# Routing worked into the attention steps of a gated cross-attention and mixture-of-experts block

## The chip, the cores and the metric

One core of a Trainium2 chip runs the whole block. The metric is device time in microseconds (us) of one launch. Each engine (PE is the matrix engine, DVE the vector engine, ACT the scalar engine, POOL is GpSimd, SP issues DMAs) runs its own list of instructions strictly in order, and the engines meet only at semaphores.

## The reference, cut to what matters

```
x = x + tanh(g_xattn) * cross_attention(layernorm(x), ctx, Wq, Wk, Wv, Wu, bu, q/k norm weights)
x = x + tanh(g_ffn)   * moe(layernorm(x), Wg, W1, b1, W2, b2, Ws1, bs1, Ws2, bs2)

cross_attention: q, k, v = projections to 16 heads x 64; q and k are layer-normed per head;
                 softmax(q k^T / 8) v per sequence of 64; then the output projection and bu
moe:             probs = softmax(h @ Wg); the 2 best of 8 experts, weights normalised to sum 1
                 out = sum of weight * (silu(h @ W1[e] + b1[e]) @ W2[e] + b2[e])
                       + 0.1 * (silu(h @ Ws1 + bs1) @ Ws2 + bs2)
```

There are 64 sequences of 64 tokens, so 4096 tokens, in 32 tiles of 128. The model width is 128, the hidden width of an expert 512, all in float32; a projection is three matmuls (high x high, high x low, low x high) with operands split into parts.

## The kernel before, in words

**Attention steps.** The loop `steps` runs `step(s)` for s from -5 to 36 on four engines, written out in full. In one step each engine works on several tiles at once, shifted by a few steps: PE transposes q and k of tile s, takes its scores, and attends to tile s-1. The order inside a step is the order of the calls in that engine's `step`; nothing else schedules it. Names used below: `project_v(j, t)` is half j of the value projection of tile t, three matmuls on L981 to L983; `transpose_probabilities(j, t)` (L1017) turns the softmax of tile t and waits for POOL's `normalise_rows(t)` (L588) through `p_ready`; `values` (L399) copies v out of PSUM on ACT; `high_part` (L360) and `low_part` (L560) split the tokens; `expert_weights` on ACT (L427) rounds a slice of W1 to its high part, and `expert_weights` on POOL (L600) subtracts it for the low part, waiting through `w1hi_ready`; `second_rstd` (L546, L548) and `newton_step` (L573 to L582) make inverse roots for the norms; `scale` (L715) on DVE applies them before the transposes of q and k; `residual` (L691) adds the attention result to x and frees PE's bank (`y_read`).

**W1.** In step 1 ACT issues the DMAs of all of W1, W2 and the shared expert's weights (L346 to L352). The slices of W1 are split on ACT in call `expert_weights(s + 2)` and on POOL in call `expert_weights(s - 3)` of the same step: POOL asks for a slice that ACT has done five steps ago.

**Group stage.** After the last attention step 8 groups of 4 tiles follow (`group`). For each: second norm (L773), transposes (L1110), logits in split parts (L1118), softmax and choice of two experts by some 35 small DVE operations, the rank of each token among those of its expert (L1146 to L1149), row copies (L860), and 8 indirect DMAs on POOL (L627) that scatter the rows into `routed`. The row buffer has two slots, so DVE waits for the scatters of two groups ago (`f_sent`). The shared expert runs beside it (L1125 to L1137 on PE, L467 on ACT, L795 and L797 on DVE).

**Routed stage.** From the counts DVE works out a schedule of 39 row tiles of 256 rows, each of one expert; SP loads them, PE runs them (first hidden matmul L1176), POOL scatters results, and a last part gathers and adds them.

## Time and profile before

| what | us |
|---|---|
| median of 3 runs | 764.32 (762.17 to 764.89) |
| the profiled execution | 764.29 |
| its span, first to last instruction | 762.5 |
| first softmax transpose to the last attention step's, tiles 0 to 31 | 63 to 428 |
| groups of the router and shared expert | about 440 to 563 |
| first to last routed tile | about 582 to 740 |

A profile row gives the start, the busy time, the engine, the source line, the operation with what it writes and reads, and in square brackets how long the engine had been idle and what released it. The mean granted clock of PE over the span is 0.913 of full speed.

### The profile page before, as it was taken

The numbers are of one execution on the slowest core, as the hardware profiler recorded it, in microseconds if no ns is written. First come the engines' busy times: TensorE is split into PE (matmuls) and PEld (weight loads), VectorE is DVE, ScalarE is ACT, GpSimd is POOL, SyncE is SP. The second block draws the span as 40 slices with busy tenths as digits, with TensorE's granted clock in tenths as the row PEclk, the third lists the DMA queues.
The fourth block names the chain that finished last, engine by engine and source line by source line (L and its number), as shares of the span: only waits on it lengthen the run. The fifth ranks groups of instructions, "written<-read, shape, count | busy, mean of one in ns | idle before, by whom it ended". The sixth has DMA issues, their size and how long they took to land.

```text
span 762.5 us, 21522 instructions
## 1 busy us (share of the span) xinstructions
PE 613.7 (80%) x7702; PEld 532.5 (70%) x7702; DVE 482.2 (63%) x1189; ACT 457.1 (60%) x964; POOL 365.3 (48%) x712
## 2 busy tenths in 40 slices
PE   1718989999999999999998579786834998988860
PEld 0517777777787787877877567675733998988860
DVE  4635877878887888888877366654552444444327
ACT  3517787878888888888888233433312454444425
POOL 3422455555655555556555234555452554544450
PEclk9978999999999999999999768888865999999995
DMA  7062000000000000000000040111024222222218
GB/s 251 32 224 54 3 30 3 3 29 3 30 3 2 30 3 30 3 4 2 3 1 3 2 78 28 36 39 38 28 66 74 70 68 67 74 71 67 64 48 325
DMA packets 30037, 37.90 MB, mean 50 GB/s; under 512 B 4992, under 2 KB 20624, under 8 KB 29808
## 3 DMA queue, kind: packets, MB, share of 16 engines
q1 hardware_dynamic: 20800, 21.42, 9.2%
q0 software_dynamic: 4720, 9.89, 3.9%
q10 hardware_dynamic: 4416, 5.25, 2.5%
q8 instruction: 62, 1.02, 0.6%
q14 instruction: 39, 0.32, 0.1%
HBM read 23.13 MB, written 13.42 MB: 48 GB/s over the span
## 4 chain that ended last, share of the span: by engine, by line
PE 56%; DVE 11%; ACT 11%; issue 8%; another core or an unknown queue 5%; POOL 3%; DMA 3%; ACTq 2%; SPq 0%; DVEq 0%; POOLq 0%
PE ps L1008 8%; PE ps L1190 8%; PE ps L981 6%; PE ps L983 5%; PE ps L982 5%; PE ps L1017 4%; PE ps L1034 4%; ACT prob L406 4%; PE ps L1049 4%; PE ps L1178 3%; PE ps L1176 3%; ACT qk_T L391 3%; PE ps L1177 3%; ACTq L351 1%
## 5 line engine op out<-in xcount | busy, mean ns | idle before, releaser
L644 POOL DMA_INDIRECT results<-spo,xs_ix x78 | 75.8, 972 | 87.3 <-DVE spo L955 70.8
L708 DVE TENSOR_REDUCE ss<-wide 128x16 f32<-128x1024 f32 x64 | 78.1, 1220 | 58.5 <-ACT wide L367 48.3
L496 ACT ACTIVATE qk_T<-ps,b_cols 128x256 f32<-128x256 f32 x156 | 61.8, 474 | 77.0 <-PE ps L1178 75.5
L391 ACT ACTIVATE qk_T<-ps,lnw 128x512 f32<-128x512 f32 x128 | 96.8, 788 | 14.4 <-issue 13.1
L981 PE MATMUL ps<-w_hi,xc_hi 128*128 128x512 f32 x192 | 91.1, 475 | 13.7 <-POOL xc_lo L560 9.6
L1008 PE MATMUL ps<-ident,wide 128*128 128x128 f32 x512 | 75.9, 281 | 30.7 <-ACT qk_T L391 29.9
L1008 PEld LDWEIGHTS ps<-ident,wide 128*128 128x128 f32 x512 | 57.7, 142 | 56.9 <-ACT qk_T L391 43.0
L627 POOL DMA_INDIRECT routed<-w_raw,slot x64 | 62.2, 971 | 70.6 <-issue 53.0
L715 DVE TENSOR_TENSOR wide<-ps,rstd 128x512 f32<-128x512 f32 x128 | 81.6, 679 | 2.9 <-POOL rstd L582 2.8
L367 ACT ACTIVATE wide<-ps 128x512 f32<-128x512 f32 x128 | 77.3, 606 | 7.1 <-PE ps L983 7.1
L983 PE MATMUL ps<-w_hi,xc_lo 128*128 128x512 f32 x192 | 77.2, 402 | 0.0
L982 PE MATMUL ps<-w_lo,xc_hi 128*128 128x512 f32 x192 | 76.8, 400 | 0.0
L1190 PE MATMUL ps<-w_sb,qk_T 128*128 x624 | 76.0, 275 | 0.0
L1190 PEld LDWEIGHTS ps<-w_sb,qk_T 128*128 128x128 f32 x624 | 72.9, 192 | 0.0
L1063 PEld LDWEIGHTS ps<-wu_sb,spo 128*128 128x128 f32 x512 | 63.5, 196 | 5.3 <-ACT spo L421 2.8
L1063 PE MATMUL ps<-wu_sb,spo 128*128 128x128 f32 x512 | 64.2, 280 | 2.5 <-ACT spo L421 2.5
L588 POOL TENSOR_TENSOR prob<-prob,rinv 128x1024 f32<-128x1024 f32 x32 | 61.0, 1906 | 9.2 <-DVE rinv L744 9.2
L1176 PE MATMUL ps<-w_lo,w_hi 128*128 128x256 f32 x156 | 49.6, 318 | 10.1 <-DVE w_lo L926 10.1
L926 DVE TENSOR_TENSOR w_lo<-ps,w_lo 128x256 fp32r<-128x256 f32 x39 | 16.6, 425 | 59.4 <-ACT w_lo L487 48.7
L981 PEld LDWEIGHTS ps<-w_hi,xc_hi 128*128 128x128 f32 x192 | 37.1, 193 | 20.9 <-DVE w_lo L671 11.2
L737 DVE TENSOR_REDUCE sm<-prob 128x16 f32<-128x1024 f32 x32 | 39.1, 1221 | 17.6 <-ACT prob L406 17.6
L560 POOL TENSOR_TENSOR xc_lo<-xc_in,xc_hi 128x256 fp32r<-128x256 f32 x32 | 24.1, 754 | 52.9 <-ACT xc_hi L360 52.9
(175 smaller groups left out, 1445.6 us busy)
## 6 DMA issues: line engine op xcount, KB each, us to landing
v_sb<-routed SPq DMA_DIRECT2D x39, 129.0 KB
xc_in<-in_x SPq DMA_DIRECT2D x8, 256.0 KB, 2.8
xc_in<-in_ctx SPq DMA_DIRECT2D x8, 256.0 KB, 3.2
w_raw<-in_L_ffn_W ACTq DMA_DIRECT2D x1, 2048.0 KB, 9.2
wide<-results SPq DMA_DIRECT2D x4, 512.0 KB, 4.8
w_raw<-results SPq DMA_DIRECT2D x4, 512.0 KB, 8.2
out_x<-x_res SPq DMA_DIRECT2D x8, 256.0 KB, 4.1
x_res<-in_x SPq DMA_DIRECT2D x1, 1792.0 KB, 8.6
```

The lines of the kernel that those rows point to most:

```text
L367: nc.scalar.activation(sq[:, n, j * 512:j * 512 + 512], ps[2 * n + j][:, :], ACT.Square, scale=HD ** -0.5).then_inc(sq_ready[n][j], 1)
L391: nc.scalar.activation(qk_T[:, n, 4 * j:4 * j + 4, :].rearrange("p a n -> p (a n)"), ps[6 + j][:, :], ACT.Identity, bias=lnw[:, 2 * n + 1: ...
L644: gp_.indirect_dma_start(out=results[:, :], out_offset=bass.IndirectOffsetOnAxis(ap=xs_ix[:, b4, a:a + 1], axis=0), in_=yb[:, b4, a, :], i ...
L708: nc.vector.tensor_reduce(ss[:, n, :], sq[:, n, :].rearrange("p (h d) -> p h d", h=HEADS), AX.X, ALU.add).then_inc(ss_ready[n], 1)
L715: nc.vector.tensor_tensor(qk_n[:, n, j * 512:(j + 1) * 512].rearrange("p (h d) -> p h d", h=8), ps[2 * n + j][:, :].rearrange("p (h d) -> ...
L981: nc.tensor.matmul(out_bank, xc_hi[:, t % 2, src, :], w_hi[:, w, cols[j]], start=True, stop=False)
L982: nc.tensor.matmul(out_bank, xc_hi[:, t % 2, src, :], w_lo[:, w, cols[j]], start=False, stop=False)
L983: return nc.tensor.matmul(out_bank, xc_lo[:, t % 2, src, :], w_hi[:, w, cols[j]], start=False, stop=True)
L1008: last = nc.tensor.transpose(ps[6 + j][:, a * P:(a + 1) * P], qk_n[:, n, c0:c0 + P], ident[:, :])
L1063: last = nc.tensor.matmul(ps[7][:, 0:D], o_T[:, p, :, :].rearrange("p b n -> p (b n)"), wu_sb[:, p, :], start=(p == 0), stop=(p == PAIRS - 1))
L1176: nc.tensor.matmul(h, w_hi_c, xs_hi[:, n % 2, :], start=True, stop=False)
L1190: last_ = nc.tensor.matmul(ps[4 + n % 2][:, a * D:(a + 1) * D], hT[:, n % 2, c, a * P:(a + 1) * P], w2e[:, c, :], start=(c == 0), stop=(c ...
```

## The change

The second norm, the transposes, the logits, the choice of experts and the scatters leave the group stage and become calls inside the attention steps; routing works on batches of 8 tiles (`BT`), three batches inside the steps and the fourth after them. Rows have 130 columns instead of 129, and all 32 tiles of them are kept (`rows_all`), so no slot is waited for. The logits use one float32 matmul of a tile. The token parts have four slots (`XD`) instead of two. W1 is loaded by SP expert by expert into two slots and split in 27 parts, in steps 3 to 29. The shared expert has a stage of its own, straight-line, beginning in step 32. The calls inside each `step` stand in another order on all four engines.

```diff
@@ ACT
-            for at in w1_slices(s, s):
-                nc.scalar.activation(w1_hi_cols[:, at], w1_raw_cols[:, at], ACT.Copy).then_inc(w1hi_ready, 1)
+            e, cols = w1_part(s)
+            sc.wait_ge(w1_in[e % 2], 16 * (e // 2 + 1))
+            nc.scalar.activation(w1_hi[:, e, cols], w1_raw[:, e % 2, cols], ACT.Copy).then_inc(w1hi_ready, 1)
...
             def step(s):
...
+                values(1, s)
+                high_part(s + 4)
+                expert_weights(s)
                 probabilities(0, s - 1)
                 probabilities(1, s - 1)
-                expert_weights(s + 2)
...
@@ POOL
             def expert_weights(s):
                 if s in W1_STEPS:
-                    gp_.wait_ge(w1hi_ready, s - (STEADY.start - 1))
+                    e, cols = w1_part(s)
+                    gp_.wait_ge(w1hi_ready, s - W1_FIRST + 1)
...
+            def scatter(t):
+                if has(t):
+                    gp_.wait_ge(f_slot, t // BT + 1)
+                    for c in range(2):
+                        gp_.indirect_dma_start(out=routed[:, :], ...
...
             def step(s):
-                variance(0, s)
-                newton_step(0, s)
-                normalise_rows(s - 2)
-                output_bias(s + 1)
+                scatter(s - SCATTER_LAG)
                 variance(1, s)
                 newton_step(1, s)
-                expert_weights(s - 3)
+                output_bias(s - 2)
+                token_eps(s + 1)
+                expert_weights(s)
+                low_part(s + 3)
                 second_rstd(s - 3)
...
+                variance(0, s + 1)
+                newton_step(0, s + 1)
+                normalise_rows(s - 1)
@@ DVE
             def step(s):
+                sum_squares(0, s + 1)
+                scale(1, 0, s)
+                row_sums(s - 1)
+                row_inverses(s - 1)
+                route(s, 12)
...
                 residual(s - 2)
...
@@ PE
             def step(s):
...
+                transpose_probabilities(0, s - 1, before_p)
+                transpose_probabilities(1, s - 1, before_p)
+                scores(s)
+                attend(s - 1)
...
+                project_qk(1, 0, s + 2)
+                transpose_qk(1, 1, s + 1, before_k)
+                project_v(1, s + 1)
+                project_qk(0, 0, s + 3)
...
+            shared_result(0)
+            for g in range(1, GROUPS):
+                if g + 2 < GROUPS:
+                    transpose_tokens(g + 2)
+                if g + 1 < GROUPS:
+                    shared_hidden(g + 1)
+                if g == 1:
+                    ranks(NB - 1)
+                shared_result(g)
@@ SP
+            def load_expert(e):
+                if e >= 2:
+                    sp.wait_ge(ffw_ready, len(W1_PARTS) * (e - 1))
+                sp.dma_start(w1_raw[:, e % 2, :], w1[e, :, :] if e < E else ws1).then_inc(w1_in[e % 2], 16)
```

`route(s, 12)` on DVE runs, for a batch, 2 small operations in the first of five successive steps, then 8, 6, 12 and 4, each waiting for the one before it; the batches lie in steps 12 to 16, 20 to 24 and 28 to 32.

On PE, the end of one step and the beginning of what follows. In the kernel before, the last two projections of a step's middle are followed by the transposes of the softmax (`ps<-ident,prob`):

```order
L1008 MATMUL ps<-ident,wide 128x128 [waits kn_ready1,y_read]
L1008 MATMUL ps<-ident,wide 128x128 x3
L981 MATMUL ps<-w_hi,xc_hi 128x512 [waits kn_ready0,xlo_ready]
L982 MATMUL ps<-w_lo,xc_hi 128x512
L983 MATMUL ps<-w_hi,xc_lo 128x512
L981 MATMUL ps<-w_hi,xc_hi 128x512 [waits qn_ready0,xlo_ready]
L982 MATMUL ps<-w_lo,xc_hi 128x512
L983 MATMUL ps<-w_hi,xc_lo 128x512
L1017 MATMUL ps<-ident,prob 128x128 [waits p_ready,kT_ready0]
```

There the first projection is of k and the value projections come much earlier in the step. The same place in the changed kernel, where the first three matmuls after the transposes are `project_v(1, s + 1)`:

```order
L1052 MATMUL ps<-ident,wide 128x128 [waits kn_ready1,y_read]
L1052 MATMUL ps<-ident,wide 128x128 x3
L1020 MATMUL ps<-w_hi,xc_hi 128x512 [waits lg_ready]
L1021 MATMUL ps<-w_lo,xc_hi 128x512
L1022 MATMUL ps<-w_hi,xc_lo 128x512
L1020 MATMUL ps<-w_hi,xc_hi 128x512 [waits qn_ready0,xlo_ready]
L1021 MATMUL ps<-w_lo,xc_hi 128x512
L1022 MATMUL ps<-w_hi,xc_lo 128x512
L1061 MATMUL ps<-ident,prob 128x128 [waits p_ready,kT_ready0]
```

The value projection of half 1 has moved to the end of the step, one projection ahead of the softmax transposes.

On ACT, around the split of W1 (`w1_hi`). Before, it follows the two copies of the transposed softmax (`spo<-ps`):

```order
L399 ACTIVATE v_sb<-ps4 128x512 [waits o_done1,v_done0]
L367 ACTIVATE wide<-ps3 128x512 [waits ss_ready1,k_done1]
L391 ACTIVATE qk_T<-ps6,lnw 128x512 [waits s_done,kt_done0]
L391 ACTIVATE qk_T<-ps7,lnw 128x512 [waits s_done,kt_done1]
L367 ACTIVATE wide<-ps2 128x512 [waits ss_ready1,k_done0]
L413 ACTIVATE spo<-ps6 128x512 [waits o_done1,pt_done0]
L413 ACTIVATE spo<-ps7 128x512 [waits o_done1,pt_done1]
L427 ACTIVATE w1_hi<-w1_raw 128x160 [waits ffw_in]
```

The same place on ACT in the changed kernel:

```order
L383 ACTIVATE qk_T<-ps6,lnw 128x512 [waits s_done,kt_done0]
L359 ACTIVATE wide<-ps2 128x512 [waits ss_ready1,k_done0]
L383 ACTIVATE qk_T<-ps7,lnw 128x512 [waits s_done,kt_done1]
L391 ACTIVATE v_sb<-ps5 128x512 [waits o_done1,v_done1]
L352 ACTIVATE xc_hi<-xc_in 128x256 [waits v_done1,c_loaded1]
L419 ACTIVATE w1_hi<-w1_raw 128x176 [waits w1_in0]
L405 ACTIVATE spo<-ps6 128x512 [waits o_done1,pt_done0]
L405 ACTIVATE spo<-ps7 128x512 [waits o_done1,pt_done1]
```

The split now stands behind the copy of v, half 1, and ahead of the copies of the softmax.

On POOL, around its half of the split (`w1_lo`) and the scaling of the softmax rows (`prob<-prob,rinv`). Before:

```order
L588 TENSOR_TENSOR prob<-prob,rinv 128x1024 [waits rinv_ready]
L594 TENSOR_TENSOR x_res<-x_res,tgbu 128x128 [waits bn_done,tgbu_ready]
L568 TENSOR_SCALAR var_eps<-ss,eps 128x16 [waits ss_ready1]
L573 TENSOR_TENSOR newton<-root 128x16 [waits root_ready1]
L575 TENSOR_TENSOR newton<-newton,var_eps 128x16 [waits nw_step1]
L577 TENSOR_SCALAR newton<-newton 128x16 [waits nw_step1]
L582 TENSOR_TENSOR rstd<-root,newton 128x16 [waits kn_ready1,kn_ready0,nw_step1]
L600 TENSOR_TENSOR w1_lo<-w1_raw,w1_hi 128x160 [waits w1hi_ready]
```

The changed kernel, from its half of the split to the scaling of the rows:

```order
L609 TENSOR_TENSOR w1_lo<-w1_raw,w1_hi 128x176 [waits w1hi_ready]
L569 TENSOR_TENSOR xc_lo<-xc_in,xc_hi 128x256 [waits xhi_ready]
L555 TENSOR_TENSOR ve_2<-mv_2,eps 128x1 [waits mv2_ready]
L557 TENSOR_TENSOR rstd_2<-ve_2,expo 128x1 [waits ve2_ready]
L577 TENSOR_SCALAR var_eps<-ss,eps_q 128x16 [waits epsq_ready,ss_ready0]
L582 TENSOR_TENSOR newton<-root 128x16 [waits root_ready0]
L584 TENSOR_TENSOR newton<-newton,var_eps 128x16 [waits nw_step0]
L586 TENSOR_SCALAR newton<-newton 128x16 [waits nw_step0]
L591 TENSOR_TENSOR rstd<-root,newton 128x16 [waits qn_ready1,qn_ready0,nw_step0]
L597 TENSOR_TENSOR prob<-prob,rinv 128x1024 [waits rinv_ready]
```

The row scaling that PE's next step begins with now stands behind POOL's half of the split in the same call of `step`, with eight operations between them; before, it stood ahead of it.

## Rows read from the trace of the kernel before

**Rows 1.** Windows: busy time per engine (count), granted clock, DMA share, GB/s.

```profile
core 0: us, PE busy (x) PEld busy (x) DVE busy (x) ACT busy (x) POOL busy (x), PEclk, DMA share, GB/s
200.00:300.00 100.00, 96.09 (x1595) 80.01 (x1586) 82.77 (x144) 85.11 (x179) 57.56 (x146) 1.00 0.04 13
440.00:563.00 123.00, 95.15 (x574) 83.16 (x572) 69.68 (x365) 45.12 (x63) 58.08 (x62) 0.78 0.15 42
```

**Rows 2.** Timeline of PE in one attention step.

```profile
203.89 1.98 PEld L1063 LDWEIGHTS ps<-wu_sb,spo 128*128 128x128 f32 x16
...
209.11 0.39 PE L982 MATMUL ps<-w_lo,xc_hi 128*128 128x512 f32 x1
...
209.34 0.40 PE L983 MATMUL ps<-w_hi,xc_lo 128*128 128x512 f32 x1
...
209.70 0.85 PEld L1017 LDWEIGHTS ps<-ident,prob 128*128 128x128 f32 x8 [0.40 <-issue]
...
210.72 1.16 PE L1034 MATMUL ps<-qk_T 64*64 64x64 f32 x64
...
211.71 1.11 PE L1049 MATMUL ps<-spo,v_sb 64*64 64x64 f32 x64
```

**Rows 3.** Timeline of the same step, ACT and what it waits for.

```profile
203.89 0.39 PE L983 MATMUL ps<-w_hi,xc_lo 128*128 128x512 f32 x1
...
204.38 0.42 ACT L360 ACTIVATE xc_hi<-xc_in 128x256 fp32r<-128x256 f32 x1 [0.99 <-PE ps L983]
...
207.09 0.59 ACT L399 ACTIVATE v_sb<-ps 128x512 f32<-128x512 f32 x1
...
210.39 1.08 ACT L413 ACTIVATE spo<-ps 128x512 f32<-128x512 f32 x2 [0.40 <-PE ps L1017]
...
211.37 0.34 ACT L427 ACTIVATE w_hi<-w_raw 128x160 fp32r<-128x160 f32 x1
```

**Rows 4.** Timeline of POOL in the same steps.

```profile
202.02 0.53 POOL L600 TENSOR_TENSOR w_lo<-w_raw,w_hi 128x160 fp32r<-128x160 f32 x1
...
202.78 0.57 POOL L548 TENSOR_TENSOR rstd<-ve,expo 128x1 f32<-128x1 f32 x1
...
204.88 0.73 POOL L560 TENSOR_TENSOR xc_lo<-xc_in,xc_hi 128x256 fp32r<-128x256 f32 x1 [1.24 <-ACT xc_hi L360]
...
205.59 0.33 POOL L568 TENSOR_SCALAR var_eps<-ss,eps_q 128x16 f32<-128x16 f32 x1
...
206.61 0.22 POOL L573 TENSOR_TENSOR newton<-root 128x16 f32<-128x16 f32 x1 [0.69 <-ACT root L382]
...
207.50 0.22 POOL L582 TENSOR_TENSOR rstd<-root,newton 128x16 f32<-128x16 f32 x1
...
207.68 1.91 POOL L588 TENSOR_TENSOR prob<-prob,rinv 128x1024 f32<-128x1024 f32 x1
...
219.45 1.91 POOL L588 TENSOR_TENSOR prob<-prob,rinv 128x1024 f32<-128x1024 f32 x1
```

**Rows 5.** Windows after three long waits of PE, columns as in rows 1.

```profile
429.00:437.00 8.00, 6.00 (x83) 5.35 (x81) 0.00 (x0) 2.05 (x4) 0.00 (x0) 0.51 0.01 2
548.70:551.80 3.10, 3.10 (x8) 2.44 (x9) 1.63 (x4) 0.00 (x0) 0.00 (x0) 0.50 0.07 21
582.70:589.20 6.50, 5.95 (x26) 5.37 (x27) 1.61 (x4) 2.93 (x8) 0.00 (x0) 0.50 0.26 61
```

**Rows 6.** Timeline: a small DVE operation of the router.

```profile
460.77 0.22 DVE L880 TENSOR_REDUCE w_raw<-w_raw 128x8 f32<-128x64 f32 x1
```

**Rows 7.** Timeline: ACT's queue held by a DMA issue in step 1.

```profile
45.80 11.18 ACTq L351 DMA_DIRECT2D w_sb<-in_L_ffn_Ws  x1
```

**Rows 8.** Timeline from the second last softmax transpose to the first routed tile.

```profile
418.74 1.06 PE L1017 MATMUL ps<-ident,prob 128*128 128x128 f32 x8 [0.72 <-POOL prob L588]
...
454.04 3.65 PEld L1137 LDWEIGHTS ps<-w_sb,wide 128*128 128x128 f32 x32 [0.64 <-ACT wide L467]
...
463.47 0.99 POOL L627 DMA_INDIRECT routed<-w_raw,slot  x1 [0.30 <-issue]
...
584.38 0.58 PE L1176 MATMUL ps<-w_lo,w_hi 128*128 128x256 f32 x1
```

**Rows 9.** Groups of instructions, window 444 to 563: count, busy, mean ns, idle before.

```profile
L795 DVE SCALAR_TENSOR_TENSOR prob<-ps,tg,x_res 128x512 f32<-128x512 f32 x7 | 5.3, 751 | 33.5 <-remote 32.6 <-PE ps L1137 0.9
```

More of the change, by code:

```diff
@@ L27 @@
 GN = GT * P
-ROW = D + 1
+ROW = D + 2
+BT = 8
+NB = TILES // BT
+XD = 4
 RT = 256
@@ L254, in eps_of, with batch_at @@
             return eps_q[:, t % 4:t % 4 + 1] if n == 0 else eps[:, 1, 0:1]
-        def groups(eng, group):
-            for g in range(2):
-                group(g, g, False)
-            with eng.Fori(0, GROUPS // 2 - 2) as i:
-                for half in range(2):
-                    group(2 * i + (2 + half), half, False)
-            for g in range(GROUPS - 2, GROUPS):
-                group(g, g % 2, g == GROUPS - 1)
+        def batch_at(s, lag):
+            b, at = divmod(s - lag, BT)
+            return (b, at) if 0 <= b < NB - 1 else (None, 0)
         def r_slot(n):
@@ new lines, in logits, with ranks @@
+            def logits(t):
+                if has(t):
+                    if has(t + 4):
+                        pe.wait_ge(sub_ready[1], t + 5)
+                    else:
+                        pe.wait_ge(lg_ready, t)
+                    if t == 0:
+                        pe.wait_ge(wg_in, 16)
+                    pe.wait_ge(rT_ready, t + 1)
+                    nc.tensor.matmul(ps[5][:, 0:E], row_T[:, t % 2, :], wg_raw[:, :], start=True, stop=True).then_inc(lg_done, 1)
+            def ranks(b):
+                pe.wait_ge(f_cnt, b + 1)
+                nc.tensor.matmul(ps[5][:, E:2 * E], before[:, :], cnt_b[:, b, :], start=True, stop=True)
+                nc.tensor.matmul(ps[5][:, 2 * E:3 * E], ones_b[:, :], cnt_b[:, b, :], start=True, stop=True).then_inc(f_rank, 1)
@@ new lines, in route_ranks, with transpose_tokens @@
+            def route_ranks(s, lag):
+                b, at = batch_at(s, lag)
+                if b is not None and at == 3:
+                    ranks(b)
+            def transpose_tokens(g):
+                pe.wait_ge(norm_ready, GT * g + GT)
+                if g == 0:
+                    pe.wait_ge(sub_ready[0], TILES)
+                else:
+                    pe.wait_ge(f_lo, g)
+                for j in range(GT):
+                    last = nc.tensor.transpose(ps[4][:, j * P:(j + 1) * P], rows_all[:, GT * g + j, 0:D], ident[:, :])
+                last.then_inc(f_t, 1)
@@ new lines, in shared_result @@
+            def shared_result(g):
+                pe.wait_ge(act_ready, CH * (g + 1))
+                if g >= 1:
+                    pe.wait_ge(f_x2, 2 * g - 1)
+                else:
+                    pe.wait_ge(o_ready[0], TILES)
+                for j in range(GT):
+                    for c in range(CH):
+                        last = nc.tensor.matmul(ps[6][:, j * D:(j + 1) * D], act[:, g % 2, c, j * P:(j + 1) * P], w2_sb[:, E, c, :],
+                                                start=(c == 0), stop=(c == CH - 1))
+                last.then_inc(fy_done, 1)
@@ L1151, in _ @@
-            transpose_tokens(0, 0)
-            pe.wait_ge(ffw_ready, len(W1_STEPS) + 2)
-            pe.wait_ge(w2_in, 3 * 16)
-            pe.wait_ge(y_read, TILES)
-            logits(0)
-            groups(pe, group)
+                project_qk(0, 1, s + 2)
+                transpose_qk(0, 0, s + 1, before_q)
+                logits(s - 4)
+                route_ranks(s, 12)
+                transpose_qk(0, 1, s + 1, before_q)
+                project_qk(1, 1, s + 2)
+                project_v(0, s + 1)
```

625 lines of the change are left out of this document (322 added, 303 removed).

## Prediction

> **What bounds the kernel now.** I read the windows first. In the attention steps PE is busy 96 of 100 us at full clock, DVE 83, ACT 85, POOL 58; in the group stage PE is busy 95 of 123 us at a granted clock of 0.78 [rows 1]. So PE bounds the first stage and something else the second. The timeline gives the pace of the first: POOL's row scaling comes again after 219.45 - 207.68 = 11.77 us [rows 4]. For the second, the groups of instructions say what is late: DVE sat idle 33.5 us ahead of the shared expert's sum, 32.6 of them released by nothing on the core, which are the scatters of two groups before [rows 9]. A scatter takes 0.99 us and the next follows 0.30 later, 1.3 us each [rows 8], so the 64 of them are 83 us of the stage. From the second last softmax transpose (tile 30, at 418.74) to the first routed hidden matmul (584.38) pass 165.6 us [rows 8]. That stretch is what the change attacks.
>
> **Part 1: the stage after attention.** What stays in it is PE's work for the shared expert. A hidden layer is 12 matmuls 0.23 us apart (209.11 to 209.34) [rows 2], 2.8 us. A result is 3.65 us [rows 8], four transposes are 0.4 (8 in 0.85) [rows 2]. After tile 30's transposes come: the rest of its step, 7 us of PE; transposes, high and low part of the first group, and its hidden layer, 6; then tile 31's softmax, attention, projection and the norm and logits of the last tiles, a chain over ACT, DVE and PE of some 10. That is 23. From there 8 results, 6 hidden layers and 5 times four transposes are 29.2 + 16.8 + 2.0 = 48 us. DVE has the last batch to route in between: 32 small operations of about 0.25 (0.22 for one [rows 6], plus the hand-over), the clearing of the pads (3 to 4 us, on POOL before), the schedule (6), so it holds PE by some 8 us at results 1 to 3: 56. The hand-over to the first routed tile is 3 (a sum on DVE, a transpose, its two parts). 23 + 56 + 3 = 82 against 165.6, **-84 us**. POOL's remaining scatters don't set the end: 16 of the last batch after its places, 38 us in, take 21, with landing and loading the rows 65 of the 82. At both ends: PE's pauses there might cost clock, 15 us (-69); if DVE holds nobody, -95. The stretch from tile 28 to 30 gets 2 longer (three tiles at the end of the loop ran at less than 11.77), and the first routed tiles no longer start at clock 0.50, which stood for 6.5 us [rows 5], worth -3. Taken: **-85**.
>
> **Part 2: the wait that the new order makes.** This is where I expect the result to be decided. POOL's `expert_weights(s)` asks for the slice that ACT splits in its own `expert_weights(s)`. In ACT's step s this stands behind `values(1, s)`, which needs `project_v(1, s)`, and PE does that almost at the end of its step s-1. In POOL's step s it stands ahead of `normalise_rows(s - 1)`, and PE's step s begins with waiting for those rows. `low_part(s + 3)`, next to it, asks for a part that ACT made one step earlier, `high_part(s + 4)`; the split has no such distance. Before, ACT was five steps ahead. So in steps 3 to 29 PE's last value projection and its next softmax transposes are joined by a chain that nothing can overlap, since both ends are PE's own and everything between is in order. Its length, in the order in which it runs:
> - end of the projection to ACT's copy: 0.10 (203.89 + 0.39 to 204.38); the copy 0.49 (one takes 0.59, two 1.08); `high_part` 0.33 (0.42 less the same overlap of 0.09); the split 0.36 (0.34 for 160 columns, now up to 176) and 0.08 to POOL, as between L360 and L560: 1.36 [rows 3, 4].
> - POOL: its split and the first operation of `second_rstd` 0.80 (202.02 to 202.78, and 0.04 for the columns); `low_part` 0.71 (204.88 to 205.59); the power 0.60; `variance` 0.33; Newton 0.89 (206.61 to 207.50) and 0.18; the row scaling 1.91 and 0.11 to PE (to 209.70): 5.53 [rows 2, 4].
>
> Together 6.9 us. Only one projection lies in it, and it too waits until POOL's Newton and DVE's `scale` are through. PE's own part, from the softmax transposes to the end of the value projection, is 0.85 + 1.0 scores + 1.05 attention + 5 projections at 0.69 and 0.17 of drain + 16 transposes 1.7 + the output projection 1.98 + new: one transpose 0.11 and the logits 0.25, and 0.1 for a drain on ACT = 10.65 [rows 2]. A step is 17.5 us instead of 11.77. **27 x 5.75 = +155.** The bounds are tight, since each term is a row: 147 to 165. Outside steps 3 to 29 PE needs 11.3 us with its new work where it had some 1 us of pauses in 11.77; I take nothing for it.
>
> **Part 3: PE's clock.** In each such step PE now waits 5.6 us, runs one projection, and waits another 0.4. After long waits the clock stood at half: 0.50 for 3.1 us of work from 548.7, for 6.5 us from 582.7, 0.51 for the 8 us from 429 [rows 5]. With pauses under 1 us it is 1.00 [rows 1]. The projection starts the work 1.2 us ahead of the transposes, so 1.9 to 5.3 us of the step proper run at half, which costs half of that, 0.95 to 2.65; I take the middle, 1.9 with the projection's own share. **27 x 1.9 = +51**, with 0 and 75 as ends. The Trainium skill, in "TensorE: Matmul & The Clock Gate", section "HAM oscillation — how this bites in real kernels", says that an array that waits between bursts starts every burst throttled and that the penalty is half of the throttled time. By that rule this term is there in every one of the 27 steps; by the attention rows alone, which never leave 1.00, it would be 0.
>
> **Part 4: routing inside the steps.** DVE runs 2, 8, 6, 12 and 4 small chained operations of 0.25 us in five steps of a batch [rows 6], ahead of `residual`, which PE waits for before `transpose_qk(1, 1, ...)`. The cover there is about 0.5 us (the residual can be done at 8.7 of the step, PE asks at 9.3). What sticks out: 0, 1.5, 1.0, 2.5 and 0.5 = 5.5 a batch, three batches, **+16** (12 to 22). It lies ahead of the value projection, so the wait of part 2 doesn't hide it. The scatters (two a step, 2.6 us on POOL) and the row and logit copies are hidden: POOL and DVE stand still for over 5 us in each of these steps anyway. Without part 2 they would matter: POOL's 58% plus 22% is still under PE.
>
> **Part 5: W1 by SP.** ACT's queue is held 11.18 us in step 1 by a DMA issue behind 4.6 MB of weights [rows 7], and PE waits. Half of the bytes leave that queue. Between 0 and -9 us; taken **-5**.
>
> **Sum**, on the profiled execution's 764.3 us (span 762.5, 1.8 around it; it is the median of the runs): 764.3 - 85 + 155 + 51 + 16 - 5 = **896 us**.
>
> **Rivals.**
> - *The wait isn't there*, because the step counters of ACT and POOL don't line up as I read them, and the steps stay at about 11.6 us. Then 764.3 - 85 + 16 - 5 = 690 us, and the change wins clearly. It decides if ACT's split comes over 7 us ahead of PE's softmax transposes. For it: POOL and ACT have slack in the profile and everything else in the new order lines up within a step. Against it: the waits and the order above say otherwise. 0.07.
> - *The clock stays up*: the projection inside the pause is enough work to hold 1.00. 845 us. For it: 0.7 us of full-rate matmul after 5.6 of pause; against it the 0.50 after pauses of 3 us at the end of attention. 0.20.
> - *The clock doesn't come back within a step*, as from 429 to 437 [rows 5]. PE's 10.65 us are then nearly doubled, where ACT doesn't hold it anyway: some 8 more per step instead of 1.9, 1060 us. 0.05.
>
> **How the numbers follow.** My forecast has 0.68. The range takes in the second rival at its upper bounds and the ends of part 3: 840 to 940. A measurement of this kernel can tell 0.5% from no change. Faster by that: the first rival, 0.07; the same 0.01, as no case lies near 764; slower 0.92.
>
> **What would show it.** In the profile after: POOL's split of W1 idle before it for over 4 us, released by ACT's split; PE's softmax transposes idle before them with POOL's row scaling as releaser, 27 times; the row scaling every 17.5 to 20 us in steps 3 to 29 and about 11.5 in the two after; PE's clock in the steps between 0.7 and 0.9; the stretch from tile 30's transposes to the first routed tile near 82 us. If the row scaling comes every 12 us, part 2 is wrong and the kernel is faster. If the pace is 17.5, part 3 is.

## The result, and the profile after

The changed kernel takes 905.57 us (median of 4 runs, 902.04 to 908.83) against 763.25 for the kernel before on the same chip: a ratio of 1.188, with a 95% interval of 1.184 to 1.192. Forecast were 896 us and a range of 840 to 940. The profiled execution took 908.83 us with a span of 907.1.

Windows of the changed kernel; columns as in [rows 1], the length of the window behind its bounds:

```profile
200.00:300.00 100.00, 70.03 (x1033) 59.08 (x1034) 53.58 (x114) 55.02 (x116) 34.41 (x88) 0.84 0.04 12
625.09:728.85 103.76, 74.15 (x647) 66.46 (x645) 44.87 (x118) 36.92 (x60) 35.20 (x38) 0.89 0.18 46
```

In the attention steps PE was busy 96 of 100 us at full clock [rows 1]; now 70 at 0.84, and every other engine is down with it. No engine has become the bound: something holds all of them in turn. The second window reaches from tile 30's softmax transposes to the first routed hidden matmul. It is 103.8 us where it was 165.6 [rows 8]. With these marks the two spans can be taken apart exactly: up to tile 30's transposes 625.09 - 418.74 = **+206.4 us**, from there to the first routed tile 103.8 - 165.6 = **-61.9**, the rest 178.3 against 178.1, **+0.1**. Together +144.6, the difference of the spans.

The timeline shows what holds the engines. This is the changed kernel at the end of one PE step, between PE's last value projection and its next softmax transposes, to be laid beside [rows 3, 4]:

```profile
229.54 0.40 PE L1022 MATMUL ps<-w_hi,xc_lo 128*128 128x512 f32 x1
229.99 0.60 ACT L391 ACTIVATE v_sb<-ps 128x512 f32<-128x512 f32 x1
230.47 0.42 ACT L352 ACTIVATE xc_hi<-xc_in 128x256 fp32r<-128x256 f32 x1
230.78 0.34 ACT L419 ACTIVATE w_hi<-w_raw 128x160 fp32r<-128x160 f32 x1
231.20 0.52 POOL L609 TENSOR_TENSOR w_lo<-w_raw,w_hi 128x160 fp32r<-128x160 f32 x1 [8.68 <-ACT w_hi L419]
231.68 0.73 POOL L569 TENSOR_TENSOR xc_lo<-xc_in,xc_hi 128x256 fp32r<-128x256 f32 x1
...
233.19 0.33 POOL L577 TENSOR_SCALAR var_eps<-ss,eps_q 128x16 f32<-128x16 f32 x1
...
234.39 0.22 POOL L591 TENSOR_TENSOR rstd<-root,newton 128x16 f32<-128x16 f32 x1
234.57 1.90 POOL L597 TENSOR_TENSOR prob<-prob,rinv 128x1024 f32<-128x1024 f32 x1
234.64 0.69 DVE L713 TENSOR_TENSOR wide<-ps,rstd 128x512 f32<-128x512 f32 x1 [6.59 <-POOL rstd L591]
...
235.48 0.77 PE L1020 MATMUL ps<-w_hi,xc_hi 128*128 128x512 f32 x1 [5.55 <-DVE wide L713]
...
236.90 0.84 PE L1061 MATMUL ps<-ident,prob 128*128 128x128 f32 x3
```

Read the starts downwards: the projection ends at 229.94, ACT copies it out, rounds the tokens, rounds W1's slice; POOL had been idle 8.68 us until just that came, and goes through its list to the row scaling; the transposes follow at 236.90. From end to start that is 6.96 us, and up to the row scaling these steps come one behind the other. The row scaling ends at 236.47; the last 0.4 us up to the transposes are the query projection of PE itself, which began at 235.48. The bracket on PE names DVE's scaling as releaser, and DVE's names POOL's Newton result: the profile names the last link of a chain each time, and only POOL's bracket names the link that was new.

Groups of the changed kernel over the whole span (line, engine, operation, count, then busy us and mean ns, then idle before and its releasers) show how often:

```profile
L609 POOL TENSOR_TENSOR w_lo<-w_raw,w_hi 128x176 fp32r<-128x176 f32 (+1 forms) x27 | 14.7, 544 | 242.2 <-ACT w_hi L419 242.2
L1020 PE MATMUL ps<-w_hi,xc_hi 128*128 128x512 f32 x192 | 99.2, 517 | 162.4 <-DVE wide L713 153.2 <-POOL xc_lo L569 9.2
L1061 PE MATMUL ps<-ident,prob 128*128 128x128 f32 x256 | 59.0, 409 | 5.7 <-ACT qk_T L383 5.6
```

It happens 27 times, one for each slice. The step can be read from the row scaling, which in [rows 4] came again after 11.77 us:

```profile
215.32 1.90 POOL L597 TENSOR_TENSOR prob<-prob,rinv 128x1024 f32<-128x1024 f32 x1
234.57 1.90 POOL L597 TENSOR_TENSOR prob<-prob,rinv 128x1024 f32<-128x1024 f32 x1
```

19.25 us here. Plain steps take 18.3 to 19.7 us (mean 18.9 over the second to the eleventh), longer where the half clock lasts longer; steps with routing take 19.1 to 22.2, and the three behind the 27th slice take 12.9, 14.9 and 15.7, with the third batch's routing in them.

### The profile page after: what moved, and what is told of

It is laid out like the page before. It is cut to its first block, busy times and chain, and to the rows that moved or that the text cites. A ratio compares the mean times of both kernels' runs of the same rounds, so it can differ in the third digit from the quotient of the medians.

```text
span 907.1 us, 21117 instructions
## 1 busy us (share of the span) xinstructions
PE 646.7 (71%) x7614; PEld 563.9 (62%) x7614; DVE 469.9 (52%) x1043; ACT 456.4 (50%) x980; POOL 360.8 (40%) x705
## 4 chain that ended last, share of the span: by engine, by line
PE 55%; DVE 15%; POOL 10%; issue 7%; ACT 7%; another core or an unknown queue 3%; DMA 1%; ACTq 1%; POOLq 0%; DVEq 0%; SPq 0%
PE ps L1274 7%; PE ps L1061 6%; PE ps L1078 6%; PE ps L1020 5%; PE ps L1052 4%; PE ps L1108 4%; PE ps L1022 4%; PE ps L1021 4%; DVE wide L713 3%; PE ps L1093 3%; PE ps L1260 2%; PE ps L1262 2%; PE ps L1176 2%; POOL xc_lo L569 2%
## 5 line engine op out<-in xcount | busy, mean ns | idle before, releaser
L1020 PE MATMUL ps<-w_hi,xc_hi 128*128 128x512 f32 x192 | 99.2, 517 | 162.4 <-DVE wide L713 153.2
L713 DVE TENSOR_TENSOR wide<-ps,rstd 128x512 f32<-128x512 f32 x128 | 87.6, 685 | 177.8 <-POOL rstd L591 177.8
L1020 PEld LDWEIGHTS ps<-w_hi,xc_hi 128*128 128x128 f32 x192 | 40.0, 208 | 180.8 <-issue 166.1
L405 ACT ACTIVATE spo<-ps 128x512 f32<-128x512 f32 x64 | 38.0, 598 | 197.3 <-PE ps L1061 196.9
L609 POOL TENSOR_TENSOR w_lo<-w_raw,w_hi 128x176 fp32r<-128x176 f32 (+1 forms) x27 | 14.7, 544 | 242.2 <-ACT w_hi L419 242.2
L504 ACT ACTIVATE qk_T<-ps,b_cols 128x256 f32<-128x256 f32 x156 | 61.9, 475 | 79.5 <-PE ps L1262 70.9
L1052 PE MATMUL ps<-ident,wide 128*128 128x128 f32 x512 | 80.0, 283 | 19.3 <-DVE x_res L689 17.9
L1022 PE MATMUL ps<-w_hi,xc_lo 128*128 128x512 f32 x192 | 84.3, 439 | 0.0
L706 DVE TENSOR_REDUCE ss<-wide 128x16 f32<-128x1024 f32 x64 | 77.5, 1212 | 12.9 <-ACT wide L359 12.3
L1021 PE MATMUL ps<-w_lo,xc_hi 128*128 128x512 f32 x192 | 83.9, 437 | 0.0
L359 ACT ACTIVATE wide<-ps 128x512 f32<-128x512 f32 x128 | 76.2, 596 | 12.7 <-issue 7.1
L721 DVE TENSOR_REDUCE mx<-ps 128x8 f32<-128x512 f32 x64 | 41.2, 686 | 72.2 <-PE ps L1078 72.2
L615 POOL DMA_INDIRECT routed<-rows_all,slot x64 | 64.4, 1007 | 22.5 <-issue 16.5
L1061 PE MATMUL ps<-ident,prob 128*128 128x128 f32 x256 | 59.0, 409 | 5.7 <-ACT qk_T L383 5.6
L1061 PEld LDWEIGHTS ps<-ident,prob 128*128 128x128 f32 x256 | 52.3, 218 | 16.6 <-ACT qk_T L383 6.5
```

The costliest lines, as they stand in the source:

```text
L359: nc.scalar.activation(sq[:, n, j * 512:j * 512 + 512], ps[2 * n + j][:, :], ACT.Square, scale=HD ** -0.5).then_inc(sq_ready[n][j], 1)
L706: nc.vector.tensor_reduce(ss[:, n, :], sq[:, n, :].rearrange("p (h d) -> p h d", h=HEADS), AX.X, ALU.add).then_inc(ss_ready[n], 1)
L713: nc.vector.tensor_tensor(qk_n[:, n, j * 512:(j + 1) * 512].rearrange("p (h d) -> p h d", h=8), ps[2 * n + j][:, :].rearrange("p (h d) -> ...
L1020: nc.tensor.matmul(out_bank, xc_hi[:, t % XD, src, :], w_hi[:, w, cols[j]], start=True, stop=False)
L1021: nc.tensor.matmul(out_bank, xc_hi[:, t % XD, src, :], w_lo[:, w, cols[j]], start=False, stop=False)
L1022: return nc.tensor.matmul(out_bank, xc_lo[:, t % XD, src, :], w_hi[:, w, cols[j]], start=False, stop=True)
```

## The experiments

The theory: in one step, POOL waits for what ACT makes in the same step behind PE's last product of the step before, ahead of what PE needs first (theory A of the first run). The rivals: the steps are long because of the work moved into them; and, for the sizes, that the clock or the routing carries another share than I gave it. Chips differ here, so every run is compared with the kernel before on its own chip. That one took 763 us in the comparison above (whether on the same chip as the next is not known), 755 in the first four runs, 718 in the next four and 716 in the last four; why is a question of its own, below.

**One step of distance put back**

```diff
@@ POOL, step
-                expert_weights(s)
+                expert_weights(s - 1)
```

> The changed kernel with one number changed: in POOL's step s the subtraction that makes W1's low part takes the slice of step s - 1, which ACT split a whole step earlier, instead of that of step s. Theory A (the same-step hand-over ACT to POOL costs the 27 steps): the row scaling comes every 11.6 to 12.5 us in steps 3 to 29, PE's clock in the windows from 200 to 400 is 1.00, POOL's idle time ahead of the subtraction falls from 242 us to under 20, and the time is about 905 - 155 - 51 = 700 us (690 to 725). Theory B (the steps are long because of what else was moved into them: routing, transposes, logits, scatters): 880 us or more, and the pace stays above 17 us. Theory C (the wait goes, but a second one of the new order stands right behind it): 740 to 850 us.

721.14 us, 0.954 of the kernel before (0.947 to 0.961). The changed kernel would be at 1.188 x 755 = 897 us on this chip, an estimate: it was not run there. The profiles agree with it: behind the last row scaling the changed kernel takes 273.5 us in the first comparison and these four runs take 265 to 267, 8 less, as the kernel before is 8 us faster here. So the one number is worth about 176 us. The group of POOL's split and that of PE's projection in this kernel:

```profile
L609 POOL TENSOR_TENSOR w_lo<-w_raw,w_hi 128x176 fp32r<-128x176 f32 (+1 forms) x27 | 14.9, 551 | 0.0
L1020 PE MATMUL ps<-w_hi,xc_hi 128*128 128x512 f32 x192 | 90.8, 473 | 13.8 <-POOL xc_lo L569 9.2 <-DVE wide L713 3.8 <-issue 0.4
```

242.2 us of idle time have become 0.0, and PE's 153.2 behind DVE have become 3.8. Before the first batch is routed the row scaling comes every 11.2 us in most steps. Theory A holds, with 721 us inside its 690 to 725; the rival, that the moved work makes the steps long, is out: the same work is there. The steps with routing, though, now take 12.9 to 16.9 us, of which later.

**The pause filled**

```diff
+            def filler(s):
+                if s + 1 in W1_STEPS:
+                    pe.wait_ge(v_ready[1], s + 2)
+                    for _ in range(18):
+                        nc.tensor.matmul(ps[5][:, :], w_hi[:, 2, 0:P], w_hi[:, 2, cols[1]], start=True, stop=True)
...
                 project_v(1, s + 1)
+                filler(s)
                 project_qk(0, 0, s + 3)
```

> The changed kernel, with 18 matmuls more on PE (0.23 us each at full clock, into a bank that nobody reads, work that the kernel does not need) between the last value projection's hand-over and the first query projection, in each of the 27 steps, so that the pause of 5.6 us is filled but not shortened. Theory A (part 3 of the prediction: the half clock behind the pause costs 1.9 us a step): granted clock above 0.95 in the windows from 200 to 400, first transposes behind the row scaling at 0.85 us instead of 1.9, time 905 - 51 = 855 us (845 to 870). Theory B (the clock is low but what waits behind those matmuls is not PE): clock near 1.00, time within 8 us of 905. Theory C (the added matmuls run at half clock themselves, 8.3 us instead of 4.1, and stick out of the pause): over 905, up to 990 us.

873.89 us, 1.157 (1.149 to 1.165): 23 us less than 897, a smaller gain than theory A gave with its 845 to 870 us. The clock in the windows of 100 us from 100 to 600 is 1.00, 0.97, 1.00, 1.00 and 0.95, where it was 0.80 to 0.84. First PE behind such a pause in the changed kernel, then the same lines in this one:

```profile
216.23 0.76 PE L1020 MATMUL ps<-w_hi,xc_hi 128*128 128x512 f32 x1 [5.59 <-DVE wide L713]
...
217.65 1.91 PE L1061 MATMUL ps<-ident,prob 128*128 128x128 f32 x8
219.48 1.95 PE L1078 MATMUL ps<-qk_T 64*64 64x64 f32 x64
```

```profile
111.87 4.36 PE L1206 MATMUL ps<-w_hi 128*128 128x512 f32 x18 [0.70 <-ACT v_sb L391]
116.74 0.47 PE L1020 MATMUL ps<-w_hi,xc_hi 128*128 128x512 f32 x1 [0.51 <-DVE wide L713]
...
117.87 1.06 PE L1061 MATMUL ps<-ident,prob 128*128 128x128 f32 x8 [0.20 <-POOL prob L597]
118.86 1.16 PE L1078 MATMUL ps<-qk_T 64*64 64x64 f32 x64
...
122.00 0.46 PE L1093 MATMUL ps<-spo,v_sb 64*64 64x64 f32 x14 [1.18 <-issue]
```

The added matmuls (L1206) leave the wait in place and take the clock from half to full: transposes and scores together take 2.2 instead of 3.9 us. Six of the ten plain steps take 17.3 to 17.4 us, against a mean of 18.9, so the clock costs up to 1.5 us a step, 27 x 1.5 = 40. The other four take 17.7 to 18.8, and in three of them PE stands idle for 0.7 to 1.2 us at an "issue" (the last row), of which the changed kernel has one in the same time. That may be a price of the experiment, which gives PE 972 more instructions (486 matmuls and as many weight loads), but no run shows it: the last run below, which adds none, has 6.0 us of the same waits. The last row scaling starts 27.9 us earlier (605.7 against 633.6), or 23.8 earlier than in the repetition of the changed kernel below (629.5). So the clock is worth 24 to 28 us as measured, and up to 40 if those waits and all else above 17.4 us are the experiment's own. The wait itself is what is left: 17.4 against 11.2 us in the run above.

**Routing behind the residual sum**

```diff
@@ DVE, step
+                if s != TILES:
+                    residual(s - 2)
                 route(s, 12)
                 if s == TILES:
                     lo_part(0)
-                residual(s - 2)
-                if s == TILES:
+                    residual(s - 2)
                     lo_part(1)
```

> The changed kernel with DVE's routing operations of a step placed behind the residual sum instead of ahead of it, all else as it is, the same-step wait too. Theory A (part 4: the routing holds the residual, and so PE, in the steps in which it runs): the four or five steps of a batch fall to about the pace of plain steps (18.3 to 19.3 us), 905 - 16 = 889 us (883 to 895). Theory B (behind the residual the same operations hold the scaling of the next queries instead): within 4 us of 905, and the steps of a batch stay at 20 to 22 us.

880.44 us, 1.165 (1.157 to 1.174), 16.6 less than 897. By the last row scaling the gain is 22.8 us (610.8 against 633.6), or 18.7 against the repetition. The steps with routing fall from 19.1 to 22.2 us to 18.3 to 19.9. PE's waits for DVE's residual sum, 17.9 us between 60 and 640 us in the changed kernel, are gone, and nothing longer has come in their place, since the operations now lie in the time in which DVE waits for POOL anyway (6.59 us at 234.64 above).

**Both edits**

> Both edits of the two experiments, the low part of W1 one step later on POOL and the routing behind the residual sum on DVE. If the two costs add, 700 - 16 = 684 us (675 to 700), and faster than the kernel before by some 80 us. If the routing is hidden by the wait of part 2 in one and sticks out in the other, the difference between this and the first alone shows it: 0 if it costs nothing without the wait, up to 22 us.

705.39 us, 0.933 (0.926 to 0.940), 15.7 less than the first edit alone, 14.9 by the last row scaling. So the order is worth about the same with and without the wait. But it is not all that routing costs. What PE waits for most in the window from 180 to 260 us, in the run with the distance alone and then with both edits (in us, in total, times, longest):

```profile
PE ps L1052 <- DVE x_res L689: 11.0, 4, 3.7
```

```profile
PE ps L1021 <- DVE wide L713: 9.2, 4, 3.4
```

Behind the residual sum the same operations hold the scaling of the queries. The steps of the first batch take 12.2, 15.1, 13.5, 16.3 and 13.0 us in this kernel, plain early ones 11.2; DVE is busy 89 of 100 us in the window from 200 to 300, and little place is left to hide them.

**Padding behind the scatters; scatters held; one scatter moved**

```diff
@@ first: SP
             sp.wait_ge(pad_ready, 2)
+            sp.wait_ge(f_sent, 16 * 2 * TILES)
@@ second: POOL, behind the steps
+            gp_.wait_ge(fy_done, GROUPS)
             for t in range(LAST_STEP - SCATTER_LAG + 1, TILES):
                 scatter(t)
@@ third: POOL, step; scatter(t, (0,)) sends the first choice's row, (1,) the second's
-                scatter(s - SCATTER_LAG)
...
                 second_rstd(s - 3)
+                scatter(s - SCATTER_LAG, (0,))
                 variance(0, s + 1)
                 newton_step(0, s + 1)
                 normalise_rows(s - 1)
+                scatter(s - SCATTER_LAG, (1,))
```

These three start from the version with both edits. They were to find the reason for something in the stage after attention. In the changed kernel's profile PE, ACT and DVE stand still there twice: for 5.44, 8.96 and 3.22 us the first time, and for 11.80, 18.49 and 10.59 us the second, the last 10.6 of them together, while POOL goes on with its scatters. From its chain of waits, and, for the first time, from its timeline:

```profile
658.43 8.94 another core or an unknown queue
...
682.33 10.73 another core or an unknown queue
```

```profile
665.47 5.21 PE L1176 MATMUL ps<-w_sb,wide 128*128 128x128 f32 x32 [5.44 <-issue]
667.39 0.60 ACT L450 ACTIVATE w_lo<-ps 128x512 fp32r<-128x512 f32 x1 [8.96 <-remote]
```

> On the version with both edits: SP waits for all scatters before it sends the padding, so that the padding (nine transfers, 17 us of SP's queue) no longer runs beside the second half of the shared expert's stage. There PE, ACT and DVE stand still for 10.65 us at 487.40, released by nothing that the trace shows, while the padding is under way; an earlier piece of 8.78 us at 463.68 has only scatters beside it. Theory A (the padding's transfers hold what the three engines wait for): the second piece goes or falls under 3 us, the first stays, the first routed tile starts up to 10 us earlier, unless the padding now ends later than PE's shared expert does: 695 to 702 against 705 us. Theory B (the scatters do it): both pieces stay, 705 us or a few more. Theory C (neither, it is the engines' own programs at these places): both pieces stay at the same instructions.

> On the version with both edits: POOL waits for the last shared result before it sends the 26 scatters that stand behind the steps, so none of them runs beside the shared expert's stage; the padding does. Theory B (scatters hold the engines): both unexplained pieces (8.8 and 10.7 us) go, PE's shared stage is 19 us shorter, and then 26 x 1.27 = 33 us of scatters are waited for: 705 - 19 + 33 = 719 us. Theory A (padding): only the second goes, about 728. Theory C: both stay, 738 us or more.

> On the version with both edits: of the two scatters that POOL sends ahead of its first variance in a step, one is moved to the middle of the step, where POOL waits 1.2 to 1.5 us for the sum of squares. Plain steps with scatters take 12.0 us and those without them 11.2. Theory A (the scatters hold POOL's Newton step, and so DVE's scaling): the later steps fall to 11.4 to 11.6, 705 - 8 = 697 us (693 to 701). Theory B (they are hidden, DVE's own load sets 12.0): within 3 us of 705.

These three ran on another chip, on which the kernel before takes 718 us. Measured: 676.51 (0.943, 0.937 to 0.949), 712.12 (0.992, 0.989 to 0.995) and 676.43 (0.945, 0.940 to 0.950). None of the three profiles has a single such piece, the two that still have scatters or padding beside the shared expert included. So these runs could not tell the theories apart, and all three were beside the point: none of them allowed that the pieces would be missing without any of the moves. The repetition below gives the value to compare with, 0.945. Against it, padding moved and one scatter moved are no difference that can be measured, and holding 26 scatters costs (0.992 - 0.945) x 718 = 34 us, which is near their 26 x 1.27 = 33: it shows that they are well hidden where they are.

**Routing spread**

```diff
@@ DVE, route, batches at 2, 3, 5, 6, 6, 6 and 4 operations
                 if at == 1:
                     expert_probabilities(b)
+                if at == 2:
                     choose(0, gp)
-                if at == 2:
+                if at == 3:
                     second_choice(b)
-                if at == 3:
+                if at == 4:
                     count(b)
+                if at == 5:
                     weigh(b)
-                if at == 4:
+                if at == 6:
                     place(b)
```

The batches now take seven steps, so the scatters come two steps later (`SCATTER_LAG` 19 instead of 17).

> On the version with both edits: the routing of a batch, 2, 8, 6, 12 and 4 small DVE operations in five steps of eight, is spread as 2, 3, 5, 6, 6, 6 and 4 over seven, the scatters two steps later. The routing steps now take 12.2, 15.1, 13.5, 16.3 and 13.0 us, the plain ones between 12.0. Theory A (each step has some slack on DVE, 1 us or so, which only the long groups exceed): the steps of a batch fall to 12.5 to 13.5, 705 - 15 = 690 us (683 to 695). Theory B (DVE is full at 12.0, so every operation costs its whole time wherever it stands): within 4 us of 705.

673.06 us, 0.940 (0.937 to 0.943), against 0.945 (0.942 to 0.948): about 4 us, less than the gain of theory A (10 to 22 us) and at the edge of B; the two intervals overlap, so it is not clear of noise. The steps of a batch became 12.2, 12.2, 13.0, 13.7, 13.5, 13.4 and 12.9, 91.0 in sum: the peaks are gone, and the others have grown. The same seven steps take 91.2 in the repetition of both edits below. So what DVE is given here it mostly pays, wherever it stands.

**The changed kernel, and both edits, again**

> The changed kernel again, unaltered, as the neighbour of the three others. On a chip on which the kernel before takes 717 us its seven unexplained pieces (5.14, 4.96, 5.31, 4.47, 5.38, 6.72 and 2.02 us, 34 in all, in the profile shown) should be missing; the changed kernel has four of them in its second stage (8.94, 10.73, 3.78 and 3.80, 27 us). If the pieces belong to the chip or to what else runs on it, the ratio is then about (905 - 27) / (763 - 34) = 1.20 and the pieces are gone; if they belong to the program, they are there on every chip and the ratio stays 1.188.

> The version with both edits again, unaltered (0.9327 of the kernel before, with unexplained pieces of 8.78 and 10.65 us, on a chip where that one took 755 us). Padding moved, one scatter moved and routing spread each gave 0.943, 0.945 and 0.940 on another chip where it took 718. If the pieces belong to the chip, this one is at 0.95 to 0.955 there, and the pieces are gone; if moving the padding did it, they are here again.

872.44 us, 1.219 (1.215 to 1.222), and 675.72, 0.945 (0.942 to 0.948), where the kernel before takes 716. Neither profile has such a piece. The attention steps are the same as on the first chip (the last row scaling starts at 629.5 us instead of 633.6); the stretch to the first routed tile is shorter by 18.9 us, and the two pieces that it lost are 19.7:

```profile
621.22:706.10 84.88, 70.07 (x648) 62.41 (x646) 44.40 (x118) 37.18 (x60) 34.95 (x38) 0.96 0.22 56
```

So the pieces belong to the chip, or to what else goes on there, and not to the program. The kernel before has seven of them, 34 us, all in its group stage, in the only profile there is of it; it is 47 us faster on these chips. The other 13 us fit as well: behind the first routed tile the changed kernel takes 165.2 us in the repetition instead of 178.3, and 763.3 - 34.0 - 13.1 = 716.2, where 716.0 was measured. That the pieces of the kernel before are gone there is such a sum and was not seen.

**All moves together**: the version with both edits, the routing spread, one scatter moved, and W2 and the shared expert's weights loaded by SP instead of ACT.

```diff
@@ ACT, load_experts
-                sc.dma_start(w2_sb[:, 0:E, :, :]. ...
-                sc.dma_start(w2_sb[:, E, :, :], ...
-                sc.dma_start(bs1_sb[:, :], bs1).then_inc(w2_in, 16)
@@ SP, in the loop over the tiles
+                if s == 1:
+                    sp.dma_start(w2_sb[:, 0:E, :, :]. ...
...
```

> Both edits, one scatter of two moved to the middle of POOL's step, routing spread over seven steps, and the loads of W2 and the shared expert's weights issued by SP in place of ACT. The spread took 434.9 - 428.3 = 6.6 us off the end of the attention steps, the scatter 0.4; ACT's square waits 7.1 us for its own engine's DMA issue in step 1, and PE 5.6 us behind that. If the loads are free on SP, that goes too: e4_both_again less 6.6 - 0.4 - 5.6 = 12.6 us (10 to 14). If SP, held by 4.6 MB in its queue, brings tokens or W1 late, the gain is 7 or less.

668.24 us, 0.934 (0.931 to 0.936), 7.5 less than both edits alone; expected were 10 to 14, and 7 or less if SP brought tokens or W1 late. From the first row scaling to the second it now takes 10.7 us instead of 18 to 19, so the held queue of [rows 7] is gone whole. Up to the last row scaling it gains 9.1 us (421.2 against 430.3), and from there to the end it takes 6 us more (245.6 against 239.7). With the routing spread alone that end takes 243.1, so a good half of the 6 goes with the spread, by which the last batches' places and scatters come later; that this is the reason was not tried.

**ACT's split first**

```diff
@@ ACT, step
             def step(s):
...
+                expert_weights(s)
                 square(1, 1, s + 1)
...
                 high_part(s + 4)
-                expert_weights(s)
```

> The changed kernel with ACT's split of W1 at the beginning of its step, ahead of the squares and of the value copy, and POOL's part unmoved (the same step, the same slice). Theory A (not the shared slice as such costs the time, but that ACT's split stands behind the copy that needs PE's last projection): the wait goes and the time is that of the lag put back, 0.954 of the kernel before; POOL's idle time ahead of its split falls from 242 us to under 20. Theory B (any hand-over within one step joins the two ends, here through the squares that stand behind it): 0.05 or more above that.

743.84 us, 1.041 (1.037 to 1.044): between the changed kernel (1.219) and the version with the distance (0.954, on another chip), so theory B by its number, though not by the squares that it named. The steps take 13.8 to 15.5 us. Three rows of its timeline say why:

```profile
173.77 0.59 ACT L391 ACTIVATE v_sb<-ps 128x512 f32<-128x512 f32 x1
174.25 0.35 ACT L419 ACTIVATE w_hi<-w_raw 128x176 fp32r<-128x176 f32 x1
...
174.68 0.57 POOL L609 TENSOR_TENSOR w_lo<-w_raw,w_hi 128x176 fp32r<-128x176 f32 x1 [4.34 <-ACT w_hi L419]
```

The split, first in its step, stands behind the last thing of the step before, the copy of the other value projection, which PE makes 4 us earlier than the last. POOL still waits, 4.34 us instead of 8.68. An engine's step has no wall at its end: to be first in it is to be behind the last of the one before.

## Why the prediction was right

**The wait (part 2, +155).** Its chain was to be 6.9 us and is 6.96, or 6.7 with the pause filled (111.16 to 117.87), where PE's own projection at half clock no longer holds the transposes. Its step at full clock was to be 17.5 and is 17.4. Against the step before, 11.77, the 27 are 27 x (17.4 - 11.77) = 152, so the term is right as it was forecast. What the wait itself costs is more: without it the step is 11.2, since the new order also does away with a pause of PE of 0.5 us in each, and 27 x 6.2 = 167 in steps without routing. One thing I had wrong in form: the transposes L1061 were to be idle, 27 times. They idle 5.7 us in all. PE waits one place earlier, at the query projection L1020, 5.55 us, and then runs straight on. I had put that projection inside the pause with a second wait of 0.4 behind it; at half clock it takes 1.42 us and covers that. I also had the two steps behind the 27th slice at about 11.5 us; they are 12.9 and 14.9, with routing in them.

**The clock (part 3, +51).** Right in kind, too large by 11 to 27: 24 to 40 by the filled pause. Half clock lasts some 5 us in a long step (216.23 to 221.25), as I allowed at most, but 3.1 in others. The Trainium skill, in "TensorE: Matmul & The Clock Gate", section "HAM oscillation — how this bites in real kernels", has it that bursts between waits start throttled; the trace agrees, at 1.91 us for eight transposes against 1.06 with the pause filled. The rival that the clock stays up is out, and so is the one that it never comes back.

**Routing in the steps (part 4, +16).** 16.6 by the third run's time, 19 to 23 by its last row scaling. But what I took of it for the version without the wait failed: the same 16, and nothing for all else that was moved in. With the wait gone, DVE's routing costs what is left as well, in both orders. The plain early steps differ by 18.9 - 11.2 = 7.7 us, 27 of them by 208, and the last row scaling of the changed kernel comes only 179.8 us later than with the distance put back (633.6 against 453.8): the wait had covered 28 us of routing and scatters. So my first rival, the change without the wait, was given 690 us; the run that is nearest to it took 721, on a chip on which the kernel before is 1% faster.

**W1 by SP (part 5, -5).** 5.9: the DMA issue holds ACT's queue for

```profile
45.33 5.27 ACTq L343 DMA_DIRECT2D w_sb<-in_L_ffn_Ws  x1
```

instead of 11.18 us [rows 7]. The time from the first row scaling to the second, in which it lies, shrinks by more, from 28.3 to 18.3 us, and PE's longest wait there from 16.0 to 5.6; what the other 4 us are was not tried.

**Attention together.** By the last row scaling (633.6 us; 453.8 with the distance; 438.9 with both edits; 426.2 in the kernel before) the 207.4 us are: wait and clock 179.8, forecast 206; the order of routing and residual 14.9, forecast 16; all else 12.7, forecast -5. The last holds the 5.9 us of the queue and the shorter plain steps (27 x 0.57 = 15) as gains, against some 30 us, an estimate, of DVE's routing and POOL's scatters, which I had as hidden. Too much and too little here nearly cancel: +219 was forecast up to tile 30's transposes (with the 2 us of part 1 for the steps ahead of them), +206.4 is measured.

**The stage after attention (part 1, -85).** Here is the error of size: -84 was forecast for the stretch of 165.6 us, -61.9 is measured. The step that failed is the reading of [rows 9]. I took DVE's 32.6 us "released by nothing on the core" for the scatters of two groups before. DVE's instruction there, the shared expert's sum, does not wait for scatters at all. One of its seven, in the kernel before, and the piece of the chain of waits that ends with it:

```profile
488.35 0.75 DVE L795 SCALAR_TENSOR_TENSOR prob<-ps,tg,x_res 128x512 f32<-128x512 f32 x1 [5.10 <-remote]
```

```profile
483.25 4.96 another core or an unknown queue
```

The 32.6 us are mostly the unexplained pieces, which have nothing to do with the order of the work, and the new stage had two of them again, 19.7 us. Where they don't occur, the stretch takes 84.9 us, and the working in part 1 (23 + 56 + 3) gave 82. So the new stage was costed right, and the pieces were charged to the old order alone. The -3 for a better clock under the first routed tiles also came to nothing: in the first 6.1 us from there the clock is 0.72 instead of 0.58, but only 0.53 in the repetition, and the rest of the kernel differs by +0.1.

Where no such piece occurs, the gain is smaller still, by an estimate: 165.6 - 34.0 = 131.6 us for the old stretch, against 84.9, is -46.8. Up to tile 30's transposes the repeated kernel is 621.22 - 418.74 = 202.5 us later, and 202.5 - 46.8 = 155.7; measured there are 872.4 - 716.0 = 156.5.

The errors, 13 us too much loss up to tile 30 and 22 and 3 us too much gain behind it, partly cancel and left +144.6 against a forecast of +132. That the time came out within 10 us is in part luck: on the other chip the same kernel loses 156.

## What to carry to other kernels

When a helper moves in a software-pipelined step, write down for each hand-over between engines how many steps lie between maker and user, and compare it with before; a distance of zero joins the last work of one step to the first of the next, and the change of one index was worth about 176 us here. Cost such a chain from rows, link by link, and look for the idle time at the link that is new, not at the engine that matters. And a wait hides other costs: what looks free in a stalled step has to be priced again for the version without the stall.

## What the runs showed of the hardware

**Stops that belong to a chip.** In both profiles of the first comparison, and in those of the first four runs, PE, ACT and DVE stand still at the same time in stages that also have scatters; the pieces of the chain of waits are 2.0 to 10.7 us long, with "another core or an unknown queue", "remote" or "issue" as releaser. In the filled pause the second of them looks otherwise: between 652 and 665 us PE goes on with single matmuls, with "issue" waits of 0.5 to 1.6 us between them. On the two chips of the other eight runs there are none, and the kernel before takes 716 to 718 us instead of 755 to 763. Some small "issue" waits of PE go with them: between 200 and 420 us the version with both edits has 3.6 us of them on the one chip and none on the other, and its plain steps with scatters beside them take mostly 11.9 to 12.0 and 11.1 to 11.6 us. Not all do: ACT's split first has 6.0 us of them on a chip without the long ones. What holds the engines is open. That it is the delivery of their instructions would fit the word "issue"; no run here shows it. For a comparison it means: the kernel before differs by 5 to 7% between chips, as much as both edits together gained, and a ratio moves too, here from 1.188 to 1.219.

**The half clock lasts differently after the same pause.** The changed kernel does the same work in each plain step, behind the same pause of 5.6 us. From 160.2 to 163.3 us the granted clock is 0.51, and from 163.4 on it is 1.00. From 102.5 to 107.5, and still from 107.6 to 108.2, it is 0.50. The step with the first takes 18.4 us, the one with the second 19.7. What decides between them no run here shows.
